# Places in a hand-set order: one offset for four sequences, or a place of its own for each

## The chip, the core and the metric

The kernel runs on one core of one Trainium2 chip. The metric is the device time of one launch, in microseconds, the median of repeated runs. A core has five engines, each with its own queue that it works off strictly in order: PE (TensorE, matmul), ACT (ScalarE), DVE (VectorE), POOL (GpSimd) and SP (SyncE, here only for DMA). They meet through semaphores: an instruction may wait until a counter has a value, and everything behind it in its queue waits with it.

## What is computed

x has four sequences of 512 tokens with 128 features. Each block adds its result to x, after a layer norm of x:

```python
x = x + attn_a(layernorm(x))    # projections, rotary, a state-space scan, gated norm
x = x + ffn(layernorm(x))       # routed feed-forward, first time
x = x + attn_b(layernorm(x))    # time mixing (k, v, r, decaying sums), then channel mixing
x = x + ffn(layernorm(x))       # routed feed-forward again, same weights
```

The feed-forward has eight experts of width 256 and a shared branch. Each token takes its two best experts by softmax, but all nine branches are computed for all tokens and weighted:

```python
hid = silu(x @ w_gate[e]) * (x @ w_up[e])
y = y + w_per_expert[:, e:e + 1] * (hid @ w_down[e])
```

Time mixing: k, v and r are projections of mixtures of h with h one token earlier; two decaying sums over time (a numerator and a denominator, kept in range by a running maximum) are divided, gated with sigmoid(r), projected and added. Channel mixing: relu squared of a 512-wide projection, projected back and gated.

## The kernel before

The first block (to about 119 us) is a phase of its own and stays as it is. Everything else is one phase, `phase_body`. Its backbone is 72 *units*: unit u is branch e = u % 9 of *slot* q = u // 9, and a slot is one sequence of one of the two feed-forwards (slots 0 to 3 the first, 4 to 7 the second). The mixings of sequence s run beside it, after slot s and before slot s + 4.

For a unit's two blocks of 128 hidden features PE makes gate and up (`gate_up`, lines 1644 to 1648, three half-precision products each, since every operand is split into a high and a low half), ACT takes Silu of gate (`gate`, line 1844), DVE multiplies with up (`hidden`, line 2033), ACT makes the high half (`high`, line 1851), POOL the low half (`low`, line 2309), and PE multiplies down two units later (`down`, lines 1671 to 1673); DVE adds that into x with the routing weight (`add`, lines 2051 and 2059) three units later. PE has two banks each for gate and up, so it runs at most one unit ahead of ACT and DVE; `down(u)` waits for the low halves of unit u and for the additions of unit u - 1.

All else is hung into that backbone by four functions `beside(u, place)`, one for each of PE, ACT, DVE and POOL. A *place* is a point within a unit of an engine's queue: on DVE for instance

```python
if u >= 3: add(u - 3)
if u < UNITS:
    beside(u, 0)
    hidden(u, 0)
    beside(u, 1)
    hidden(u, 1)
    beside(u, 2)
```

On POOL places 0 and 1 stand ahead of `low(u - 1, 1)` and `low(u, 0)`; on ACT the order is place 0, first Silu, place 1, high half of the unit before, second Silu, place 2, high half, place 3. Before the change a step of sequence s stands 9 s units after that of sequence 0: `at = u - BRANCHES * s, place`, and then `if at == (16, 0): scan_max(s)`. The steps of routing and of the input norms stand at a fixed branch of each slot.

The steps that the prediction names. Routing of slot q: `logits` (PE), `route_shift`, `route_first`, `route_second`, `route_weigh` (DVE, lines 2081 to 2108) and `route_exp` (ACT). Input of slot q: `apply_x`, `turn_x` (PE, line 1678), `high_x`, `low_x`. Weights of the branches 4 to 8: `split_high` (ACT) and `split_low` (DVE, line 2210). The time mixing of sequence s: statistics of the norms `ln_a`, `ln_b` (DVE, `stats` and `aggregate`), `ln_rstd` (POOL, lines 1478 to 1480), `normalise` (ACT, line 1868), `affine` (POOL, lines 2332 and 2335), `apply_h` makes `hn`, `turn_h`, `step`, `share` (DVE, line 2143), `key`, `receptance`, `value` (PE), `scan_max`, `bounds` and `exponentials` (ACT, with the table for Exp), `scan_den` (line 2172) and `scan_num` (line 2177), the products `first_values` (`e2v`), `second_values` (`y2v`), `denominator` and `numerator` (POOL, lines 2339 to 2360), `divide`, `attend`, `output`, `join`. Channel mixing: `turn_c`, `mix`, `hidden` on PE (line 1772), `relus`, `squares`, `values`, `sigmoid`, `gated`, `add_rkv`. The Exp of the decay (line 2005) makes `w_decay` for all scans.

ACT's functions come from tables: Silu and Exp are in different ones, and a change of function puts an `ACT_TABLE_LOAD` ahead of the instruction.

Of the kernel before, what the change touches and what calls it, by code (L numbers as in the profile page):

```python
# [14 lines left out]
SEQS, SEQ = 4, 512  # L15
# [1483 lines left out]
def phase_body(core, io, lns, moe_x):  # L1499
# [8 lines left out]
    with ExitStack() as ctx:  # L1508
# [122 lines left out]
        def _(pe):  # L1631
# [162 lines left out]
            def beside(u, place):  # L1794

                q, e = divmod(u, BRANCHES)
                if (e, place) == (0, 0) and q < SLOTS:
                    logits(q)
                for s in range(SEQS):
                    at = u - BRANCHES * s, place  # L1800
                    if at == (15, 0):
                        turn_h(s)
                    if at == (16, 0):
                        key(s)
                    if at == (18, 1):
                        receptance(s)
                    if at == (18, 2):
                        value(s)
                    if at == (22, 0):
                        output(s)  # L1810
                    if at == (25, 2):
                        turn_c(s)
                    if at == (28, 2):
                        hidden(s, 0)
                        hidden(s, 1)
                        hidden(s, 2)
                    if at == (29, 0):
                        hidden(s, 3)
                    if at == (29, 2):
                        gate_c(s)  # L1820
                    if at == (30, 1):
                        values(s, (0, 1))
                        values(s, (2, 3))
                if (e, place) == (7, 2) and q + 1 < SLOTS:
                    turn_x(q + 1)
# [15 lines left out]
        def _(act):  # L1841
# [103 lines left out]

            def sigmoid(s):
# [3 lines left out]
            def beside(u, place):  # L1950
                q, e = divmod(u, BRANCHES)
                if (e, place) == (7, 3) and q + 1 < SLOTS:
                    high_x(q + 1)
                if q + 1 < SEQS:
                    if (e, place) == (6, 3):
                        apply_x(q + 1, (0, 1))
                    if (e, place) == (7, 0):
                        apply_x(q + 1, (2, 3))
                elif q + 1 < SLOTS:
                    if (e, place) == (6, 1):  # L1960
                        apply_x(q + 1, (2, 3))
                if q == 0 and FRONT_SPLITS <= e + 2 < BRANCHES and place == 1:
                    split_high(e + 2)
                for s in range(SEQS):
                    at = u - BRANCHES * s, place
                    if at == (11, 3):
                        normalise(s, (0, 1))
                    if at == (12, 1):
                        normalise(s, (2, 3))
                    if at == (14, 1):  # L1970
                        apply_h(s, (0, 1))
                    if at == (14, 2):
                        apply_h(s, (2, 3))
                    if at == (15, 1):
                        copy_h(s)
                    if at == (18, 1):
                        bounds(s)
                    if at == (19, 0):
                        exponentials(s)
                        copy_v(s)  # L1980
                    if at == (20, 1):
                        gate_r(s)
                    if at == (24, 3):
                        apply_c(s, (0, 1))
                        apply_c(s, (2, 3))
                    if at == (26, 0):
                        copy_c(s)
                    if at == (28, 2):
                        relus(s, (0,))
                        squares(s, (0,))  # L1990
                        relus(s, (1,))
                        squares(s, (1,))
                    if at == (28, 3):
                        relus(s, (2,))
                    if at == (29, 1):
                        squares(s, (2,))
                    if at == (29, 2):
                        relus(s, (3,))
                    if at == (29, 3):
# [20 lines left out]
        def _(dve):  # L2020
# [192 lines left out]
            def beside(u, place):  # L2213
                q, e = divmod(u, BRANCHES)
                if (e, place) == (0, 0):
                    route_shift(q)
                if (e, place) == (0, 1):
                    route_first(q)
                if (e, place) == (1, 0):
                    route_second(q)  # L2220
                if (e, place) == (1, 0):
                    route_weigh(q)
                if (e, place) == (6, 0) and SEQS <= q + 1 < SLOTS:
                    apply_x(q + 1, (0, 1))
                if (e, place) == (6, 1) and q < 2:
                    stats(ln_m1, x, q + 2)
                if (u, place) == (7, 0):
                    aggregate(ln_m1, 2, veps_in)
                if (u, place) == (15, 2):
                    aggregate(ln_m1, 3, veps_in)  # L2230
                if q == 0 and FRONT_SPLITS <= e + 2 < BRANCHES and place == 2:
                    split_low(e + 2)
                for s in range(SEQS):
                    at = u - BRANCHES * s, place
# [318 lines left out]
```

## Time and profile before

| what | us |
|---|---|
| three runs | 485.51, 485.63, 485.72 |
| median of the runs | 485.63 |
| span of the profiled execution | 484.0 |
| median less span (launch and end, around the span) | 1.6 |
| PE busy | 458.8 (95%) |
| DVE, ACT, POOL busy | 392.8, 364.4, 361.0 |

The profile gives the span of one execution, from its first to its last instruction; its time outside the span is not listed, so its own time is put at the median of the runs, and the span plus 1.6 us is compared with that. PE's 95% is the time in which some matmul's row is open, and these rows overlap; how much of it is issue at full speed has to be read from the starts of the rows. The other engines each have spare time over the whole span, but they have to be read stage by stage, since the four sequences' mixings start one after the other and overlap in the middle. A row's bracket gives the idle time of the engine before it and what ended it.

### The profile page before, as it was taken

What the parts mean: (1) busy time and instruction counts of PE and PEld (TensorE: products, weight loads), DVE (VectorE), ACT (ScalarE), POOL (GpSimd) and SP (SyncE); (2) the same over time, 40 slices, a digit from 0 to 9 for tenths busy, and PEclk for the clock granted to TensorE, in tenths of its full rate; (3) what the DMA queues carried; (4) which work ended last, traced back from release to release, by engine and by line L of the source; (5) the groups of instructions that cost most, each with busy time, mean ns of one, the idle gap of its engine ahead of it and who ended that gap; (6) DMA issues with size and microseconds to landing.
All of it is one profiled execution on the core that took longest, in us unless ns stands there. A gap on an engine that the chain in (4) does not pass through costs nothing.

```text
span 484.0 us, 10598 instructions
## 1 busy us (share of the span) xinstructions
PE 458.8 (95%) x3666; PEld 317.6 (66%) x3666; DVE 392.8 (81%) x1056; ACT 364.4 (75%) x709; POOL 361.0 (75%) x413
## 2 busy tenths in 40 slices
PE   7998999998999999969999989998999999999996
PEld 6775788986456655626666756575657665766664
DVE  6899888786787859997899899979997867486765
ACT  1799989865887667945999679976897588667652
POOL 4664889998566596798788989698969683575652
PEclk9999999999899999998999999999999999999999
DMA  8001010001310000000000000000000000000000
GB/s 276 21 1 65 2 34 3 1 1 35 100 37 2 1 1 1 3 1 1 2 1 1 1 2 1 0 1 3 2 0 24 1 1 24 0 2 1 23 1 24
DMA packets 7061, 8.51 MB, mean 18 GB/s; under 512 B 608, under 2 KB 5216, under 8 KB 7008
## 3 DMA queue, kind: packets, MB, share of 16 engines
q1 hardware_dynamic: 7008, 7.83, 5.0%
q8 instruction: 30, 0.49, 0.4%
q14 instruction: 23, 0.19, 0.1%
HBM read 6.78 MB, written 1.05 MB: 16 GB/s over the span
## 4 chain that ended last, share of the span: by engine, by line
PE 45%; DVE 10%; POOL 8%; ACT 8%; issue 4%; DVEq 0%; ACTq 0%; POOLq 0%
PE bank L1644 8%; PE bank L1645 8%; PE bank L1648 8%; PE bank L1671 5%; PE bank L1672 4%; PE bank L1673 4%; DVE x L2059 3%; POOL b_hid_lo L2309 2%; DVE b_hid L2033 2%; ACT b_silu L1844 2%; PE bank L1772 1%; PE bank L1789 1%; PE bank L1714 1%; PE bank L1678 1%; ACT b_hid_hi L1851 1%
## 5 line engine op out<-in xcount | busy, mean ns | idle before, releaser
L2309 POOL TENSOR_TENSOR b_hid_lo<-b_hid,b_hid_hi 128x512 f16<-128x512 f32 x143 | 172.8, 1218 | 62.6 <-ACT b_hid_hi L1851 60.8
L2033 DVE SCALAR_TENSOR_TENSOR b_hid<-bank,b_silu 128x512 f32<-128x512 f32 x144 | 97.5, 685 | 38.1 <-ACT b_silu L1844 31.3
L1844 ACT ACTIVATE b_silu<-bank 128x512 f32<-128x512 f32 x144 | 85.7, 596 | 41.7 <-PE bank L1648 39.8
L1644 PE MATMUL bank<-x_hi,wsplit 128*128 128x512 f16 x284 | 108.9, 383 | 1.1 <-DVE b_hid L2033 1.0
L1671 PE MATMUL bank<-wsplit,b_hid_hi 128*128 128x128 f16 x576 | 100.4, 219 | 9.7 <-DVE x L2059 5.6
L1645 PE MATMUL bank<-x_hi,wsplit 128*128 128x512 f16 x284 | 108.9, 383 | 0.0
L1648 PE MATMUL bank<-x_lo,wsplit 128*128 128x512 f16 x284 | 108.6, 383 | 0.0
L1673 PE MATMUL bank<-wsplit,b_hid_lo 128*128 128x128 f16 x576 | 100.5, 219 | 0.0
L1672 PE MATMUL bank<-wsplit,b_hid_hi 128*128 128x128 f16 x576 | 100.4, 219 | 0.0
L1851 ACT CAST b_hid_hi<-b_hid 128x512 f16<-128x512 f32 x144 | 88.1, 611 | 15.7 <-DVE b_hid L2033 15.3
L2059 DVE SCALAR_TENSOR_TENSOR x<-bank,b_w_branch,x 128x128 f32<-128x128 f32 x256 | 71.5, 340 | 7.8 <-PE bank L1673 7.5
L1671 PEld LDWEIGHTS bank<-wsplit,b_hid_hi 128*128 128x128 f16 x576 | 56.4, 98 | 23.4 <-POOL b_hid_lo L2309 10.4
L1672 PEld LDWEIGHTS bank<-wsplit,b_hid_hi 128*128 128x128 f16 x576 | 56.4, 98 | 6.5 <-issue 1.3
L1673 PEld LDWEIGHTS bank<-wsplit,b_hid_lo 128*128 128x128 f16 x576 | 56.5, 98 | 0.0
L1648 PEld LDWEIGHTS bank<-x_lo,wsplit 128*128 128x128 f16 x284 | 28.1, 99 | 34.3 <-issue 1.4
L1644 PEld LDWEIGHTS bank<-x_hi,wsplit 128*128 128x128 f16 x284 | 28.6, 101 | 31.0 <-DVE b_hid L2033 5.3
L1645 PEld LDWEIGHTS bank<-x_hi,wsplit 128*128 128x128 f16 x284 | 28.0, 98 | 27.1 <-issue 5.9
L545 DVE SCALAR_TENSOR_TENSOR xbc<-bank,cols,xbc 128x511 f32<-128x511 f32 (+2 forms) x48 | 35.5, 746 | 2.4 <-ACT xbc L825 1.2
L1151 PE MATMUL bank<-causal,seg_l 128*128 128x128 f32 x128 | 17.1, 278 | 0.2 <-ACT expo L870 0.2
L1844 ACT ACT_TABLE_LOAD x13 | 16.7, 1283 | 0.2
L2185 DVE RECIPROCAL bank<-b_den_r 128x256 f32<-128x256 f32 x8 | 14.0, 1754 | 3.4 <-POOL b_den_r L2352 3.4
L1151 PEld LDWEIGHTS bank<-causal,seg_l 128*128 128x128 f32 x128 | 15.7, 192 | 1.5 <-issue 1.4
(249 smaller groups left out, 927.8 us busy)
## 6 DMA issues: line engine op xcount, KB each, us to landing
moe_raw<-in_moe SPq DMA_DIRECT2D x9, 384.0 KB, 3.1
x<-in_x SPq DMA_DIRECT2D x4, 256.0 KB, 3.9
out<-x SPq DMA_DIRECT2D x3, 256.0 KB, 2.6
rope<-in_rope SPq DMA_DIRECT2D x1, 512.0 KB, 5.9
wzx<-in_wzx SPq DMA_DIRECT2D x1, 386.0 KB, 6.3
b_w_rkvo<-in_w_rkvo SPq DMA_DIRECT2D x1, 256.0 KB, 2.7
b_w_fk<-in_w_fk SPq DMA_DIRECT2D x1, 256.0 KB, 2.8
b_w_fv<-in_w_fv SPq DMA_DIRECT2D x1, 256.0 KB, 3.5
```

The costliest lines, as they stand in the source:

```text
L545: ins = nc.vector.scalar_tensor_tensor(xbc[:, b, t0 + back:t1], conv_ps[b % 2][:, 0:SEQ - back], col(core, "conv_w", TAPS * b + TAPS - 1 - ...
L1644: nc.tensor.matmul(dst, hi, x_hi[:, q % 2, :], start=True, stop=False)
L1645: nc.tensor.matmul(dst, lo, x_hi[:, q % 2, :], start=False, stop=False)
L1648: nc.tensor.matmul(dst, hi, x_lo[:, q % 2, :], start=False, stop=True).then_inc(made, 1)
L1671: nc.tensor.matmul(dst, h_hi, d_hi, start=blk == 0, stop=False)
L1672: nc.tensor.matmul(dst, h_hi, d_lo, start=False, stop=False)
L1673: ins = nc.tensor.matmul(dst, h_lo, d_hi, start=False, stop=blk == FBLK - 1)
L1844: nc.scalar.activation(silu[:, 2 * (u % 2) + blk, :], gate_ps[blk][:, :], ACT.Silu, scale=GU_UNSCALE).then_inc(silu_ready, 1)
L1851: nc.scalar.copy(hid_hi[:, FBLK * (u % 3) + blk, :], hid[:, 2 * (u % 2) + blk, :]).then_inc(hi_ready, 1)
L2033: nc.vector.scalar_tensor_tensor(hid[:, 2 * (u % 2) + blk, :], up_ps[blk][:, :], GU_UNSCALE * H_SCALE, silu[:, 2 * (u % 2) + blk, :], ALU. ...
L2059: ins = nc.vector.scalar_tensor_tensor(x[:, i, :], down_bank(u)[:, P * c:P * (c + 1)], w_branch[:, q % 2, e, c:c + 1], x[:, i, :], ALU.mul ...
L2309: nc.gpsimd.tensor_tensor(hid_lo[:, slot, :], hid[:, 2 * (u % 2) + blk, :], hid_hi[:, slot, :], ALU.subtract).then_inc(lo_ready, 1)
```

## The change

Each step gets a list of (unit, place), one for each sequence or slot, and is called where the list says so. The branches of the old `beside` are split so that steps that stood together have lists of their own. No step is added or taken away, and their arithmetic is the same. Every engine's `beside` changes in this way; two lists of each kind are shown here.

```diff
             def beside(u, place):
-
-                q, e = divmod(u, BRANCHES)
-                if (e, place) == (0, 0) and q < SLOTS:
-                    logits(q)
+                here = u, place
+                for q in range(8):
+                    if here == ((0, 0), (7, 2), (16, 1), (27, 1), (36, 0), (44, 0), (53, 1), (61, 2))[q]:
+                        logits(q)
                 for s in range(SEQS):
-                    at = u - BRANCHES * s, place
-                    if at == (15, 0):
+                    if here == ((15, 0), (24, 0), (33, 0), (41, 1))[s]:
                         turn_h(s)
...
-                if (u, place) == (4, 0):
-                    nc.scalar.activation(w_decay[:], col(core, "decay"), ACT.Exp).then_inc(decay_act, 1)
+                for q in range(8):
+                    if here == ((0, 2), (7, 2), (19, 0), (27, 2), (36, 2), (45, 2), (53, 2), (61, 3))[q]:
+                        route_exp(q)
+                for q in range(1):
+                    if here == ((7, 3),)[q]:
+                        decay(q)
...
+                for q in range(8):
+                    if here == ((2, 0), (10, 1), (19, 0), (27, 2), (36, 2), (45, 2), (54, 0), (65, 1))[q]:
+                        route_second(q)
+                for q in range(8):
+                    if here == ((3, 1), (12, 0), (20, 1), (28, 0), (37, 0), (46, 0), (55, 0), (66, 2))[q]:
+                        route_weigh(q)
...
-                    if at == (19, 0):
+                    if here == ((18, 2), (27, 1), (36, 2), (46, 0))[s]:
                         scan_den(s)
-                    if at == (19, 2):
+                    if here == ((19, 1), (29, 0), (37, 1), (46, 1))[s]:
                         scan_num(s)
...
-                    if at == (11, 2):
+                    if here == ((11, 2), (20, 1), (29, 1), (38, 1))[s]:
                         affine(s, 0)
```

The Exp of the decay becomes a function `decay` with the same instruction. Where the order until now guaranteed that a value was there, the steps now wait for it by name:

```diff
             def divide(s, half):
                 dve.wait_ge(den_ready, s + 1)
+                dve.wait_ge(routed, s + 3)
...
             def first_values(s):
+                pool.wait_ge(expo_ready, 4 * s + 2)
                 pool.wait_ge(v_copied, s + 1)
...
             def second_values(s):
+                pool.wait_ge(expo_ready, 4 * (s + 1))
+                pool.wait_ge(v_copied, s + 1)
...
             def denominator(s, part):
                 if part == 0:
+                    pool.wait_ge(expo_ready, 4 * (s + 1))
...
             def numerator(s, part):
                 if part == 0:
+                    pool.wait_ge(expo_ready, 4 * (s + 1))
...
             def add_x4(s):
+                pool.wait_ge(x4_ready, s + 1)
```

**Where rows move.** In the rows that follow, `b_` marks a tile of this phase, `bank` is a PSUM bank, and brackets hold the semaphores that a row waits for. The lines of the changed kernel are some 3 to 28 higher than those of the kernel before.

On POOL, from the time mixing's products of sequence 0 (unit 18) on. Before:

```order
L2339 TENSOR_TENSOR b_e2v<-b_expo,b_v_sb 128x512 [waits b_v_copied]
L2342 TENSOR_TENSOR b_y2v<-b_expo,b_v_sb 128x512
L2347 TENSOR_TENSOR b_den<-b_expo,b_bb 128x512 [waits b_bb]
L2309 TENSOR_TENSOR b_hid_lo<-b_hid,b_hid_hi 128x512 [waits b_hid_hi,b_pool_step]
L2309 TENSOR_TENSOR b_hid_lo<-b_hid,b_hid_hi 128x512 [waits b_hid_hi]
L2349 TENSOR_TENSOR b_den<-b_den,b_expo 128x512
L2352 TENSOR_TENSOR b_den_r<-b_den,b_e_r 128x512 [waits b_er1,b_pool_step]
L2357 TENSOR_TENSOR b_num<-b_expo,b_aa 128x512 [waits b_aa]
L1478 TENSOR_TENSOR ln_tm_rstd<-ln_tm_veps,mhalf 128x4 [waits b_veps_a,b_pool_step]
L1479 TENSOR_TENSOR ln_tm_nbias<-ln_tm_mv,ln_tm_rstd 128x4 [waits b_pool_step]
L1480 TENSOR_SCALAR ln_tm_nbias<-ln_tm_nbias 128x4 [waits b_pool_step]
```

Now:

```order
L2374 TENSOR_TENSOR b_den<-b_expo,b_bb 128x512 [waits b_bb,b_expo]
L2363 TENSOR_TENSOR b_e2v<-b_expo,b_v_sb 128x512 [waits b_v_copied,b_expo,b_pool_step]
L2376 TENSOR_TENSOR b_den<-b_den,b_expo 128x512
L2332 TENSOR_TENSOR b_hid_lo<-b_hid,b_hid_hi 128x512 [waits b_hid_hi,b_pool_step]
L2368 TENSOR_TENSOR b_y2v<-b_expo,b_v_sb 128x512 [waits b_v_copied,b_expo]
L2379 TENSOR_TENSOR b_den_r<-b_den,b_e_r 128x512 [waits b_er1]
L2385 TENSOR_TENSOR b_num<-b_expo,b_aa 128x512 [waits b_aa,b_expo]
L2332 TENSOR_TENSOR b_hid_lo<-b_hid,b_hid_hi 128x512 [waits b_hid_hi,b_pool_step]
L1478 TENSOR_TENSOR ln_tm_rstd<-ln_tm_veps,mhalf 128x4 [waits b_veps_a]
```

The denominator's first product (`b_den<-b_expo,b_bb`) stands ahead of `b_e2v`, its second product ahead of the low half, and `b_y2v` and the numerator between two low halves; before, three products stood ahead of two low halves and three behind them, with `ln_rstd` next.

On DVE, around the denominator's scan `b_bb` of sequence 0 (units 18 and 19). Before, with the end of the routing of slot 2 ahead of it:

```order
L2106 TENSOR_TENSOR bank<-bank,b_second 128x32
L2107 SCALAR_TENSOR_TENSOR bank<-bank,b_ex 128x32 [waits b_dve_step]
L2108 TENSOR_TENSOR b_w_branch<-bank,b_best 128x4x8 [waits b_dve_step]
L2172 SCALAR_TENSOR_TENSOR b_bb<-b_expo 128x512 [waits b_expo]
L2033 SCALAR_TENSOR_TENSOR b_hid<-bank,b_silu 128x512 [waits b_hid_lo,up_made,b_silu] x2
L2177 SCALAR_TENSOR_TENSOR b_aa<-b_expo,b_e2v 128x512 [waits b_e2v]
L2059 SCALAR_TENSOR_TENSOR x<-bank,b_w_branch,x 128x128 [waits b_down]
L2059 SCALAR_TENSOR_TENSOR x<-bank,b_w_branch,x 128x128 x3
```

Now:

```order
L2177 TENSOR_SCALAR b_e_r<-bank 128x512 [waits b_r_made]
L2185 SCALAR_TENSOR_TENSOR b_bb<-b_expo 128x512 [waits b_expo]
L2072 SCALAR_TENSOR_TENSOR x<-bank,b_w_branch,x 128x128 [waits b_down]
L2072 SCALAR_TENSOR_TENSOR x<-bank,b_w_branch,x 128x128 x3
L2108 SCALAR_TENSOR_TENSOR bank<-bank,b_ex 128x32 [waits b_exp]
L2109 TENSOR_REDUCE b_best<-bank 128x4 [waits b_dve_step]
L2110 TENSOR_TENSOR bank<-bank,b_best 128x32 [waits b_dve_step]
L2111 TENSOR_TENSOR bank<-bank,b_rank 128x32 [waits b_dve_step]
L2083 TENSOR_REDUCE b_best<-bank 128x4 [waits b_dve_step]
```

The scan stands right behind `negative_r` (`b_e_r`), ahead of the additions (`x<-bank,b_w_branch,x`) and of the routing's rows, of which those of `route_weigh` have gone to unit 20.

On ACT, the Exp of the decay. Before, in unit 4:

```order
L1851 CAST b_hid_hi<-b_hid 128x512
L2005 ACT_TABLE_LOAD
L2005 ACTIVATE b_w_decay<-cols 128x1
L1844 ACT_TABLE_LOAD
L1844 ACTIVATE b_silu<-bank 128x512
```

Now, in unit 7:

```order
L1847 ACTIVATE b_silu<-bank 128x512
L1919 ACT_TABLE_LOAD
L1919 ACTIVATE b_ex<-b_shift 128x32
L1854 CAST b_hid_hi<-b_hid 128x512
L1950 ACTIVATE b_w_decay<-cols 128x1
L1847 ACT_TABLE_LOAD
L1847 ACTIVATE b_silu<-bank 128x512
```

It shares one pair of table loads with the routing's Exp (`b_ex<-b_shift`) of slot 1.

## Rows read from the trace of the kernel before

**Rows 1.** Head of the page.

```profile
span 484.0 us, 10598 instructions
```

**Rows 2.** Timeline of PE, unit 44: start us, us, engine, line, operation, tiles.

```profile
343.39 0.38 PE L1644 MATMUL bank<-x_hi,wsplit 128*128 128x512 f16 x1
343.60 0.38 PE L1645 MATMUL bank<-x_hi,wsplit 128*128 128x512 f16 x1
```

**Rows 3.** Who PE waited for: us in total, times, longest us.

```profile
PE bank L1671 <- DVE x L2059: 5.6, 9, 1.8
PE bank L1671 <- POOL b_hid_lo L2309: 4.0, 2, 3.5
...
PE bank L1678 <- ACT b_hn L1876: 1.2, 3, 0.4
PE bank L1644 <- DVE b_hid L2033: 1.0, 2, 0.8
...
PE bank L1772 <- DVE b_w_branch L2108: 0.4, 1, 0.4
```

**Rows 4.** Stages: length, busy of PE, PEld, DVE, ACT, POOL; clock, DMA, GB/s.

```profile
119.00:153.00 34.00, 31.27 (x248) 18.33 (x249) 26.24 (x71) 28.46 (x49) 20.77 (x31) 0.95 0.19 60
153.00:184.00 31.00, 30.12 (x270) 19.14 (x269) 22.93 (x79) 22.07 (x42) 23.30 (x26) 1.00 0.01 1
184.00:205.00 21.00, 20.71 (x174) 12.76 (x172) 19.70 (x62) 17.27 (x32) 14.87 (x15) 1.00 0.01 2
205.00:223.00 18.00, 12.44 (x97) 7.23 (x95) 16.05 (x30) 9.98 (x20) 17.60 (x17) 0.91 0.00 0
...
270.00:289.00 19.00, 17.57 (x149) 10.64 (x147) 17.23 (x58) 12.90 (x28) 17.10 (x21) 1.00 0.01 2
...
322.00:340.00 18.00, 16.57 (x137) 9.85 (x135) 16.54 (x56) 11.90 (x26) 16.10 (x21) 1.00 0.01 2
```

**Rows 5.** Timeline of PE: waits, with idle us and releaser in brackets.

```profile
126.38 0.39 PE L1644 MATMUL bank<-x_hi,wsplit 128*128 128x512 f16 x1 [0.75 <-DVE b_hid L2033]
...
141.30 0.22 PE L1671 MATMUL bank<-wsplit,b_hid_hi 128*128 128x128 f16 x1 [1.01 <-DVE x L2059]
...
149.67 0.22 PE L1671 MATMUL bank<-wsplit,b_hid_hi 128*128 128x128 f16 x1 [0.35 <-DVE x L2059]
...
211.05 0.22 PE L1671 MATMUL bank<-wsplit,b_hid_hi 128*128 128x128 f16 x1 [1.78 <-DVE x L2059]
...
218.59 0.23 PE L1671 MATMUL bank<-wsplit,b_hid_hi 128*128 128x128 f16 x1 [3.45 <-POOL b_hid_lo L2309]
```

**Rows 6.** Timeline of ACT, unit 4: two table loads.

```profile
133.38 1.28 ACT L2005 ACT_TABLE_LOAD   x1
...
134.90 1.28 ACT L1844 ACT_TABLE_LOAD   x1
```

**Rows 7.** Timeline of DVE, units 18 and 19.

```profile
202.24 0.18 DVE L2095 SCALAR_TENSOR_TENSOR bank<-bank,b_ex 128x32 f32<-128x32 f32 x1
...
204.87 1.64 DVE L2172 TENSOR_TENSOR_SCAN b_bb<-b_expo 128x512 f32<-128x512 f32 x1
...
207.63 2.26 DVE L2177 TENSOR_TENSOR_SCAN b_aa<-b_expo,b_e2v 128x512 f32<-128x512 f32 x1
```

**Rows 8.** Timeline of POOL, units 18 to 20.

```profile
207.54 1.26 POOL L2347 TENSOR_TENSOR b_den<-b_expo,b_bb 128x512 f32<-128x512 f32 x1
208.88 3.07 POOL L2309 TENSOR_TENSOR b_hid_lo<-b_hid,b_hid_hi 128x512 f16<-128x512 f32 x2
...
215.84 1.01 POOL L1478 TENSOR_TENSOR ln_tm_rstd<-ln_tm_veps,mhalf 128x4 f32<-128x4 f32 x1
...
217.38 1.16 POOL L2309 TENSOR_TENSOR b_hid_lo<-b_hid,b_hid_hi 128x512 f16<-128x512 f32 x1
```

**Rows 9.** Line 2177, the numerator's scans: ns, minimum, median and maximum of four.

```profile
L2177 DVE TENSOR_TENSOR_SCAN b_aa<-b_expo,b_e2v x4: 1330/1336/2257, 207.6 to 361.4; 128x512 f32<-128x512 f32 x4
```

**Rows 10.** Timeline of ACT, unit 20: normalising begins.

```profile
217.46 0.88 ACT L1868 ACTIVATE b_xn<-x,ln_tm_nbias,ln_tm_rstd 128x128 f32<-128x128 f32 x2 [5.25 <-POOL ln_tm_nbias L1480]
```

More of the change, by code:

```diff
@@ L1823, in beside @@
                         values(s, (2, 3))
-                if (e, place) == (7, 2) and q + 1 < SLOTS:
-                    turn_x(q + 1)
+                for q in range(7):
+                    if here == ((5, 0), (16, 0), (25, 1), (34, 1), (42, 1), (53, 0), (61, 1))[q]:
+                        turn_x(q + 1)
             for u in range(UNITS + 2):
@@ L1944, in squares, with decay @@
                     nc.scalar.square(sq[:, b, :], relu[:, b, :]).then_inc(sq_ready, 1)
+            def decay(_):
+                nc.scalar.activation(w_decay[:], col(core, "decay"), ACT.Exp).then_inc(decay_act, 1)
             def sigmoid(s):
@@ L1950, in beside @@
             def beside(u, place):
[L1951 to L1955, printed above, removed]
+                here = u, place
+                for q in range(7):
+                    if here == ((5, 1), (16, 1), (25, 3), (34, 3), (43, 0), (53, 1), (61, 3))[q]:
+                        high_x(q + 1)
+                for q in range(3):
+                    if here == ((3, 1), (12, 2), (20, 2))[q]:
@@ L1956, in beside @@
                         apply_x(q + 1, (0, 1))
-                    if (e, place) == (7, 0):
+                for q in range(7):
+                    if here == ((4, 2), (15, 3), (24, 2), (34, 0), (42, 0), (51, 1), (60, 1))[q]:
                         apply_x(q + 1, (2, 3))
[L1959 to L1963, printed above, removed]
+                for q in range(5):
+                    if here == ((2, 3), (3, 0), (4, 0), (4, 3), (7, 0))[q]:
+                        split_high(q + FRONT_SPLITS)
@@ L2225, in beside @@
[L2225 to L2232, printed above, removed]
+                here = u, place
+                for q in range(8):
+                    if here == ((0, 1), (7, 2), (18, 1), (27, 1), (36, 1), (44, 2), (53, 1), (61, 1))[q]:
+                        route_shift(q)
@@ L2374, in beside @@
             def beside(u, place):
-                q, e = divmod(u, BRANCHES)
-                if (e, place) == (8, 0) and q + 1 < SLOTS:
-                    low_x(q + 1)
-                if (u, place) == (9, 2):
-                    pool.wait_ge(veps_in, 1)
-                    ln_rstd(nc, core, link, ln_m1, of_seq(2), rstd_in)
-                if (u, place) == (18, 2):
-                    pool.wait_ge(veps_in, 2)
-                    ln_rstd(nc, core, link, ln_m1, of_seq(3), rstd_in)
+                here = u, place
@@ L2384, in beside @@
+                for q in range(7):
+                    if here == ((8, 0), (16, 1), (26, 0), (34, 1), (43, 1), (53, 0), (61, 2))[q]:
+                        low_x(q + 1)
+                for q in range(2):
+                    if here == ((8, 1), (15, 0))[q]:
+                        pool.wait_ge(veps_in, q + 1)
+                        ln_rstd(nc, core, link, ln_m1, of_seq(q + 2), rstd_in)
                 for s in range(SEQS):
-                    at = u - BRANCHES * s, place
-                    if at == (11, 0):
+                    if here == ((10, 2), (20, 0), (28, 2), (37, 1))[s]:
```

157 lines of the change are left out of this document (87 added, 70 removed).

## The prediction

> **What bounds the kernel now.** The profiled execution spans 484.0 us [rows 1]; the runs have a median of 485.63 us, so 1.6 us lie around the span, and I add them back at the end. First view: the timeline of PE in an undisturbed unit. Two gate matmuls that follow each other start 0.21 to 0.22 us apart although each row lasts 0.38 us [rows 2]. So a PE that shows no idle time is issuing as fast as it can, and a wait costs some 0.16 us more than the idle time that the trace shows for it (0.38 less 0.22). Second view: who PE waited for. Over the whole body five kinds hold 12.2 us: 5.6 for DVE's additions, 4.0 for POOL's low halves, the rest for ACT's `hn`, DVE's products and the routing weights [rows 3]; some 0.8 us of the 5.6 belong to the very last unit, which nothing here touches. Third view: the stages. PE lost 34.00-31.27 = 2.7 us in 119 to 153, 0.9 in 153 to 184, 0.3 in 184 to 205, 18.00-12.44 = 5.6 in 205 to 223, and 1.4 in each of 270 to 289 and 322 to 340 [rows 4]. Elsewhere in the body PE lost next to nothing. PE is therefore the bound, and the change can earn only these waits: its matmuls are the same before and after. In the worst stage POOL was busy 17.60 of 18 us and DVE 16.05; in 270 to 289 DVE had 17.23 of 19 [rows 4]. So in the stages that lose, PE waits because another engine's queue is full there, not because of one slow instruction.
>
> What is in reach: 2.1 us in three waits of the first stage (0.75, 1.01 and 0.35 [rows 5]; the other 0.6 us stands at the start of the phase, ahead of every moved step), 0.9, 5.6 and twice 1.4 us. Adding 0.16 per wait makes that 2.6, 1.2 (two waits), 6.0 (three) and twice 2.2 (five each). In 205 to 223 the mean granted clock was 0.91 [rows 4], so 0.09 of 18 us was lost to it: 1.6 us at the lower level (1.2 GHz for 3.2 us). A last wait of 0.4 us for the routing weights costs 0.5. All together **16.3 us**.
>
> **Part by part.**
>
> *Start (119 to 153), reach 2.6, taken 2.4.* ACT loads an activation table for `w_decay` in unit 4 and the Silu table again: 1.28+1.28 us [rows 6]. Now the Exp of `w_decay` stands behind the routing's Exp of unit 7, which has the table in already, so one pair leaves: 24 loads in the body where there were 26. ACT is 2.6 us earlier, and the wait at 141.30 is for an addition that stood behind a product which had waited for ACT. `route_second` and `route_weigh` leave the place ahead of unit 1's first product (now units 2 and 3): the wait at 126.38 was for that product, which now is ready some 0.8 us earlier. Two of the five `split_low` now come before their unit's products, not behind them. What is added in their place: the turn of slot 1 (four transposes) at unit 5 instead of 7, which PE does at either place. I leave 0.2 for a new wait.
>
> *Units 9 to 15 (153 to 184), reach 1.2, taken 1.2.* The statistics of `ln_a` go ahead of unit 11's first product, and the routing's 13 rows no longer stand ahead of unit 10's. So `rstd`, which POOL makes ahead of a low half, comes by more than the 0.55 us that PE waited at 171; and the second norm's `ln_rstd` moves to unit 12, so `hn` is there before PE turns it.
>
> *Units 16 to 22 (184 to 223), reach 7.6 in 205 to 223, taken 3.0.* Here one wait feeds the next. The scan of the denominator stands behind 13 routing rows, from 202.24 to 204.87 [rows 7]; POOL's first product of the denominator starts only at 207.54, and POOL then runs without a pause until the low half at 217.38, for which PE has waited 3.45 us [rows 5, 8]. In the new order the scan stands ahead of the addition and of the routing, so only ACT's two exponentials hold it: 204.87-202.24 = 2.6 us earlier, and some 0.4 more because it no longer runs beside `y2v`. POOL has idle time before 205 (14.87 of 21 us busy [rows 4]), so it can take that work about 3 us earlier, and everything behind moves up with it. The lower bound is nothing: POOL still has the same six products and three low halves, and `route_weigh` now stands ahead of `ln_a`'s statistics (1.2 us later). The upper bound is 7.6, no wait and no drop of the clock. I take 3.0, which is the time by which the row that starts POOL's run moves; the clock I leave as it is, since PE keeps a wait of some 2 us.
>
> *Sequences 2 and 3 (270 to 289, 322 to 340), reach 2.2 each, taken 1.3 each.* Without waits such a stage lasts 19.0-2.2 = 16.8 us, and DVE has 17.23 us of work in it [rows 4]; so at least 0.4 has to leave the stage. It does: the second norm's statistics and aggregation come a unit earlier, `share` two places later, and the sigmoid's table pair stands behind unit 30's first Silu. Bounds 0 and 2.2; I take 1.3, between what DVE's load allows (1.8) and half.
>
> *The wait for the routing weights, reach 0.5, taken 0.4.* The hidden product of sequence 3 goes from unit 55 to 56, the weights are made a place earlier.
>
> *New waits.* POOL waits by name for the exponentials, for `v` and for `x4`, DVE for the routing before it divides. Each names what an earlier row of the same queue, or the order until now, had guaranteed; I cost them at nothing. Behind a wait of POOL stands the next low half, and PE waits for that: this is the price if I am wrong (rival S). SP's queue is unchanged.
>
> Sum: 2.4+1.2+3.0+2.6+0.4 = 9.6 us. 484.0-9.6 = 474.4, and with 1.6 around it **476.0 us**.
>
> **Rivals.**
>
> *All of it.* If no wait is left, 16.3 us go: 467.7+1.6 = 469.3. For it: each wait has its own step moved. Against: POOL's 17.60 of 18.
>
> *The full queues keep theirs.* Then only the start, units 9 to 15 and the routing wait are won: 4.0 us, 481.6. For it: loads of 89% to 98% in the three stages. Against: the stages before them have idle time.
>
> *DVE and POOL meet more often.* The scan of the numerator took 2.26 us at 207.63 where it otherwise takes 1.33 [rows 7, 9], beside a POOL product. If the new order brings two more such meetings in each of four sequences, 8 x 0.93 = 7.4 us come back on DVE's queue: 483.4. For it: scans and mixings now stand where POOL has its own products. Against: the first scan moves to where POOL waits for it. The Trainium skill (SBUF — State Buffer, Who interferes with whom) says that a DVE instruction with two inputs in SBUF and a GpSimd instruction that reads SBUF hold the shared interface one at a time, for the whole instruction. By that rule a meeting costs up to the whole of the other instruction and the sum would be this rival's; the longer row agrees with it.
>
> *S, slower.* `affine(s, 0)` now stands ahead of POOL's low half in units 20, 29 and 38, and waits for four rows of ACT that come up to two places later. Today the normalising begins at 217.46, after 5.25 us of waiting for `rstd` [rows 10]. If it ends later than POOL is free, the low half queues behind it and PE stands as it stood at 218.59: 3.45+0.16 us and 1.6 for the clock, 5.2 in each of three sequences, 15.6 in all: 476.0+15.6 = 491.6. It decides from where normalising, four rows of some 0.44 us, ends after the work that stands ahead of `affine` on POOL. Against: PE has the hidden products of the sequence before in units 28 to 30 and 37 to 39, which cover a late low half; nothing covers unit 20.
>
> *Nothing to see.* A run cannot be told from no change within 0.2%, 1 us. If the jam of 205 to 223 only moves, and the start's gain fills PE's waits further on, the time stays at 485.6.
>
> **How the numbers follow.** Forecast 0.52 (472 to 480), all of it 0.13, full queues 0.13, meetings 0.07, S 0.10, nothing 0.05. Faster: 0.52+0.13+0.13+0.07 = 0.85; same 0.05; slower 0.10. The range reaches from 469.5 to 483.5: it holds the forecast, most of the full gain, the full queues and the meetings, and leaves out S and no change.
>
> **What would show it.** Right: no table load for `w_decay` of its own, no PE wait of a microsecond before 150; the scan of the first denominator within 0.5 us of ACT's second exponential; PE's wait in units 19 to 21 below 3 us in one piece; two waits fewer in sequences 2 and 3. Wrong: a POOL `affine` with a wait for ACT in front of it and a PE wait for a low half behind; scans above 2 us in more than one sequence; a second stretch at the lower clock in the body.

## The result, and the profile after

The changed kernel takes 479.06 us (478.16 to 479.66), the kernel before 485.68 us (485.51 to 486.04): a ratio of 0.9862, interval 0.9844 to 0.988. That is 6.6 us less; 9.6 were forecast, and 479.06 lies within 469.5 to 483.5. The profiled execution spans 477.1 us, 6.9 less than before [rows 1].

TensorE's mean granted clock differs between runs of one kernel (the kernel before took from 484.54 us at a mean clock of 1.0 to 487.06 us at 0.988 beside e1 to e4, the changed kernel from 478.16 at 0.998 to 479.66 at 0.995), so medians are compared, and half a microsecond between single runs says nothing.

The head of the page, and who PE waited for in the body (us in total, times, longest us):

```profile
span 477.1 us, 10616 instructions
```

```profile
PE bank L1671 <- DVE x L2072: 4.2, 4, 1.7
PE bank L1671 <- POOL b_hid_lo L2332: 3.1, 1, 3.1
PE bank L1644 <- DVE b_hid L2046: 1.2, 2, 0.9
PE bank L1644 <- ACT b_silu L1847: 1.0, 1, 1.0
...
```

The waits are fewer and longer than before: four for additions where there were nine, one for a low half where there were two, none for `hn` and the routing weights [rows 3]. The stages, with columns as in [rows 4], show where they went. They are fixed stretches of time: by 213 us the changed kernel is 5 us ahead, so each holds somewhat later work than it did before.

```profile
119.00:153.00 34.00, 32.11 (x273) 20.13 (x274) 26.37 (x74) 28.99 (x50) 19.53 (x31) 1.00 0.18 59
153.00:184.00 31.00, 31.00 (x279) 19.54 (x277) 26.11 (x91) 22.68 (x46) 25.08 (x29) 1.00 0.01 1
184.00:205.00 21.00, 19.96 (x165) 12.27 (x164) 19.67 (x43) 17.49 (x31) 16.98 (x15) 1.00 0.01 3
205.00:223.00 18.00, 14.65 (x117) 9.03 (x118) 16.08 (x50) 9.14 (x19) 16.20 (x19) 0.91 0.00 1
223.00:270.00 47.00, 45.55 (x373) 30.50 (x372) 44.20 (x113) 40.68 (x75) 41.67 (x39) 1.00 0.01 1
270.00:289.00 19.00, 19.00 (x175) 12.71 (x174) 17.73 (x49) 14.93 (x30) 16.79 (x20) 1.00 0.00 1
289.00:322.00 33.00, 31.31 (x249) 20.83 (x246) 31.84 (x79) 28.23 (x49) 26.76 (x26) 1.00 0.00 1
322.00:340.00 18.00, 18.00 (x159) 12.01 (x157) 17.14 (x50) 15.57 (x32) 16.83 (x18) 1.00 0.01 2
```

PE's idle time (length less busy) went from 2.73 to 1.89 us in 119 to 153, from 0.88 to 0 in 153 to 184, from 5.85 to 4.39 in 184 to 223, and from 1.43 to 0 in 270 to 289 and in 322 to 340. New are 1.45 in 223 to 270 and 1.69 in 289 to 322, where PE lost nothing before. These are the remaining large waits, in PE's timeline:

```profile
124.70 0.39 PE L1644 MATMUL bank<-x_hi,wsplit 128*128 128x512 f16 x1 [0.98 <-ACT b_silu L1847]
...
204.91 0.39 PE L1644 MATMUL bank<-x_hi,wsplit 128*128 128x512 f16 x1 [0.91 <-DVE b_hid L2046]
...
213.18 0.23 PE L1671 MATMUL bank<-wsplit,b_hid_hi 128*128 128x128 f16 x1 [3.05 <-POOL b_hid_lo L2332]
...
249.65 0.22 PE L1671 MATMUL bank<-wsplit,b_hid_hi 128*128 128x128 f16 x1 [1.45 <-DVE x L2072]
...
300.73 0.22 PE L1671 MATMUL bank<-wsplit,b_hid_hi 128*128 128x128 f16 x1 [1.69 <-DVE x L2072]
```

Two questions follow: why 3.05 of 3.45 us stayed at the low half of unit 19, and what the waits at 249.65 and 300.73, each for an addition, are.

The first: this is POOL in the new order, then in the old one. A *run* here is a row of products between which POOL does not pause.

```profile
199.34 1.27 POOL L2374 TENSOR_TENSOR b_den<-b_expo,b_bb 128x512 f32<-128x512 f32 x1 [3.03 <-DVE b_bb L2185]
200.69 1.27 POOL L2363 TENSOR_TENSOR b_e2v<-b_expo,b_v_sb 128x512 f32<-128x512 f32 x1
...
208.99 1.16 POOL L2332 TENSOR_TENSOR b_hid_lo<-b_hid,b_hid_hi 128x512 f16<-128x512 f32 x1
210.44 1.01 POOL L1478 TENSOR_TENSOR ln_tm_rstd<-ln_tm_veps,mhalf 128x4 f32<-128x4 f32 x1 [0.30 <-DVE ln_tm_veps L2144]
...
211.97 1.15 POOL L2332 TENSOR_TENSOR b_hid_lo<-b_hid,b_hid_hi 128x512 f16<-128x512 f32 x1
```

```profile
204.16 1.27 POOL L2339 TENSOR_TENSOR b_e2v<-b_expo,b_v_sb 128x512 f32<-128x512 f32 x1 [0.39 <-ACT b_v_sb L1897]
205.38 2.19 POOL L2342 TENSOR_TENSOR b_y2v<-b_expo,b_v_sb 128x512 f32<-128x512 f32 x1
```

The first product of the denominator moved from 207.54 [rows 8] to 199.34, but before the change it was not the start of POOL's run: `e2v` and `y2v` ran from 204.16 on, released by ACT's copy of `v`. Now it is the start, and waits 3.03 us for the scan. So the run starts 204.16-199.34 = 4.8 us earlier, not 8.2. From its start to the second low half of unit 19 it is 211.97-199.34 = 12.6 us now and was 217.38-204.16 = 13.2; the same products, low halves and `rstd` stand in it. In either order ACT releases it, by the copy of `v` before (203.51, now 199.01) and by the exponentials and the scan behind them now (200.90 before, 196.39 now): both came 4.5 us earlier. PE came to the low half 5.0 us earlier (at 213.18-3.05 for 218.59-3.45) and POOL 5.4 earlier, so the wait hardly changed.

The second: DVE in units 27 and 28, ACT's row that `route_second` needs, and the same addition on DVE before the change.

```profile
246.43 0.67 DVE L2046 SCALAR_TENSOR_TENSOR b_hid<-bank,b_silu 128x512 f32<-128x512 f32 x1
247.01 0.19 DVE L2108 SCALAR_TENSOR_TENSOR bank<-bank,b_ex 128x32 f32<-128x32 f32 x1
...
248.38 1.13 DVE L2072 SCALAR_TENSOR_TENSOR x<-bank,b_w_branch,x 128x128 f32<-128x128 f32 x4
```

```profile
246.46 0.21 ACT L1919 ACTIVATE b_ex<-b_shift 128x32 f32<-128x32 f32 x1
```

```profile
250.93 1.11 DVE L2059 SCALAR_TENSOR_TENSOR x<-bank,b_w_branch,x 128x128 f32<-128x128 f32 x4
```

Six rows of `route_second` (247.01 to 248.38) now stand ahead of the addition for which PE waits until 249.65; in unit 36 the same rows, `negative_r` and a scan do (296.39 to 299.49). Before, all of them but `negative_r` stood behind it. They do not wait for ACT here: its row ends at 246.67, and DVE comes to `route_second` at 247.01 without a pause. PE reaches the addition's matmul 5.4 us earlier than before (at 249.65-1.45 = 248.20 for 253.62, where it did not wait), but the addition starts only 250.93-248.38 = 2.6 us earlier.

### The profile page after: what moved, and what is told of

Same layout as the page of the kernel before. It is cut to its first block, busy times and chain, and to the rows that moved or that the text cites. A ratio compares the mean times of both kernels' runs of the same rounds, so it can differ in the third digit from the quotient of the medians.

```text
span 477.1 us, 10616 instructions
## 1 busy us (share of the span) xinstructions
PE 455.1 (95%) x3666; PEld 317.6 (67%) x3666; DVE 396.7 (83%) x1056; ACT 363.3 (76%) x707; POOL 359.0 (75%) x413
## 4 chain that ended last, share of the span: by engine, by line
PE 65%; DVE 5%; ACT 3%; issue 1%; POOL 1%; DVEq 0%; ACTq 0%
PE bank L1644 12%; PE bank L1645 12%; PE bank L1648 12%; PE bank L1671 6%; PE bank L1673 6%; PE bank L1672 6%; PE bank L1789 3%; PE bank L1772 3%; PE bank L1678 1%; PE bank L1714 1%; DVE x L2072 1%; DVE b_hid L2046 1%; PE bank L1699 1%; PE bank L1743 1%; PE bank L1779 1%
## 5 line engine op out<-in xcount | busy, mean ns | idle before, releaser
L2332 POOL TENSOR_TENSOR b_hid_lo<-b_hid,b_hid_hi 128x512 f16<-128x512 f32 x143 | 168.1, 1187 | 50.1 <-ACT b_hid_hi L1854 47.7
L1185 PE MATMUL bank<-xdt,mix 128*128 128x64 f32 x128 | 16.3, 272 | 0.2
L1095 PE MATMUL bank<-normT,wzx 128*128 128x512 f32 x32 | 16.1, 601 | 0.1
```

What stands on the lines that cost most here:

```text
L2332: nc.gpsimd.tensor_tensor(hid_lo[:, slot, :], hid[:, 2 * (u % 2) + blk, :], hid_hi[:, slot, :], ALU.subtract).then_inc(lo_ready, 1)
```

## The experiments

The parts come first, then the term of units 16 to 22, then the two places where an engine's queue may be so full that a wait only moves (a *jam*). "The changed kernel" below is 479.06 us.

**e1 and e2: the parts.** In e1 only the steps that stood in units 0 to 15 have their new place, in e2 those of units 0 to 24; `route_second` in both and `aggregate(ln_a, .)` in e2:

```diff
-if here == ((2, 0), (10, 1), (19, 0), (27, 2), (36, 2), (45, 2), (54, 0), (65, 1))[q]:
+if here == ((2, 0), (10, 1), (19, 0), (28, 0), (37, 0), (46, 0), (55, 0), (64, 0))[q]:
...
-if here == ((11, 0), (20, 2), (29, 0), (38, 0))[s]:
+if here == ((11, 0), (20, 2), (29, 1), (38, 1))[s]:
```

> Only the steps that stood in units 0 to 15 before have their new unit and place; all others stand where they stood. Theory 'terms add up' (each stage's waits are its own): the start gives 2.6 us and units 9 to 15 give 1.2, as the two traces differ there, so 485.7 - 3.8 = 481.9 us. Rival 'the jam takes it' (units 16 to 22 are set by when POOL and ACT get through, so an earlier PE only waits longer there): 484 us or more.

> The steps that stood in units 0 to 24 before have their new place, the later ones the old. Terms add up: 1.3 us below e1 (the waits of units 16 to 22 differ by that much in the two traces), 480.6 us; then the places from unit 25 on are worth only 1.5 us, as the waits that leave in sequences 2 and 3 (4.9) less two new ones (3.5). Rival: the whole of the rest lies here, 479.1 us, and the later places are worth nothing.

e1 took 483.15 us (483.11 to 484.1) and e2 481.08 (480.2 to 482.78), beside 486.02 for the kernel before. So the start and units 9 to 15 are worth 2.9 us, units 16 to 24 another 2.1, and the rest 2.0, or 1.7 if each is set against the kernel before of its own session (486.02 and 485.68). Within that the parts add up; no jam takes the first gain. e1 pays for its mixture: a wait for `share`, which still stands at its old place, and the old wait for the low half:

```profile
184.31 1.10 PE L1714 MATMUL bank<-b_shared_h,b_w_rkvo 128*128 128x512 f32 x2 [1.00 <-DVE b_shared_h L2156]
...
215.51 0.23 PE L1671 MATMUL bank<-wsplit,b_hid_hi 128*128 128x128 f16 x1 [3.46 <-POOL b_hid_lo L2332]
```

**e3: one table pair.** Every step at its old place but `decay`. (What ran is the changed kernel's code with the old places, so its named waits are in it too; they show no row of their own.)

```diff
-if here == ((4, 0),)[q]:
+if here == ((9, 3),)[q]:
```

> The kernel before with one edit: the Exp of w_decay moved behind the routing's Exp of unit 9, so one pair of table loads leaves. Theory 'ACT's 2.6 us are what PE waited for at 141.3': that wait (1.0 us, 1.2 with the pitch) goes, perhaps the one at 149.6 too (0.5): 484.0 to 484.5 us. Rival 'DVE's queue is late by itself' (routing and splits): within 0.3 us of 485.7.

485.13 us (484.46 to 486.37), ratio 0.999, interval 0.9977 to 1.0003: not told from no change. The trace has 24 table loads in the body and no wait at 141. So the wait was for ACT, as held. The profiled execution is e3's slowest (486.37 us): its stage 205 to 223 shows a mean clock of 0.82 where before had 0.91 [rows 4], 1.6 us more lost to the lower level, and the microsecond is used up there. Runs of the same mean clock differ the right way: at 0.996 the six of e3 took 484.46 to 485.38 us, the three of the kernel before 485.32 to 485.54. How much of the microsecond stays is not settled by this.

**e7: the step that sized units 16 to 22.** On e1, only the scan moved:

```diff
-if here == ((19, 0), (28, 0), (37, 0), (46, 0))[s]:
+if here == ((18, 2), (28, 0), (37, 0), (46, 0))[s]:
                         scan_den(s)
```

> e1 (483.15 us) with one step more at its new place: the scan of sequence 0's denominator, ahead of the addition and of the routing rows. The prediction held that POOL's run in units 18 to 20 starts with the scan, so the scan 2.6 us earlier is worth up to 3.0 us: 480.2 us. Rival 'the run starts with e2v, which waits for ACT's copy of v': POOL starts no sooner and has the same work, within 0.4 us of 483.15, or slower by up to 1 as the addition stands behind the scan.

482.4 us (481.51 to 483.35): 0.75 less than e1, not 3.0. PE's wait for the low half is what it was, 3.44 us for 3.46, and `e2v`, still the first of POOL's products, starts at 201.44 for 201.08. The wait for the addition fell from 1.78 to 0.86, and one for a product rose from 0.35 to 0.77:

```profile
184.27 1.10 PE L1714 MATMUL bank<-b_shared_h,b_w_rkvo 128*128 128x512 f32 x2 [0.99 <-DVE b_shared_h L2156]
...
207.41 0.22 PE L1671 MATMUL bank<-wsplit,b_hid_hi 128*128 128x128 f16 x1 [0.86 <-DVE x L2072]
...
214.94 0.29 PE L1671 MATMUL bank<-wsplit,b_hid_hi 128*128 128x128 f16 x1 [3.44 <-POOL b_hid_lo L2332]
```

In the old order of POOL an earlier scan alone does nothing for the low half. (The first row serves the section on why the prediction was right.)

**e4: the additions first.** On the changed kernel:

```diff
-if here == ((2, 0), (10, 1), (19, 0), (27, 2), (36, 2), (45, 2), (54, 0), (65, 1))[q]:
+if here == ((2, 0), (10, 1), (19, 0), (28, 0), (37, 0), (45, 2), (54, 0), (65, 1))[q]:
                         route_second(q)
...
-if here == ((18, 2), (27, 1), (36, 2), (46, 0))[s]:
+if here == ((18, 2), (27, 1), (37, 0), (46, 0))[s]:
                         scan_den(s)
```

> The changed kernel with DVE's route_second of slots 3 and 4 and the scan of sequence 2's denominator behind the additions of units 25 and 34, as before the change, in place of ahead of them. Theory 'rows that wait for ACT stand ahead of an addition that PE waits for': the new PE waits at 249.6 and 300.7 (1.45 and 1.69 us, 3.5 with the pitch) lose 1.4 and 1.85 us: 479.1 - 3.2 = 475.9 us. Rival 'DVE's queue is full there': the next products come later by as much and the waits move on: 478.5 to 479.1 us.

479.28 us: nothing. The waits for the two additions are gone, and PE waits a matmul or a unit later for the routing weights and a product:

```profile
251.10 3.67 PE L1772 MATMUL bank<-b_mixed,b_w_fk 128*128 128x512 f32 x8 [1.16 <-DVE b_w_branch L2121]
...
301.04 2.81 PE L1772 MATMUL bank<-b_mixed,b_w_fk 128*128 128x512 f32 x6 [0.53 <-DVE b_w_branch L2121]
...
310.31 0.39 PE L1644 MATMUL bank<-x_hi,wsplit 128*128 128x512 f16 x1 [0.92 <-DVE b_hid L2046]
```

3.14 us of idle time became 2.61, in three waits instead of two, and the time is the same: the rival, a full DVE queue, holds. My theory of single rows at the wrong place falls.

**e8: the scan behind as well.** e4 with sequence 1's scan behind the weights, and two POOL products with it:

```diff
-if here == ((18, 2), (27, 1), (37, 0), (46, 0))[s]:
+if here == ((18, 2), (28, 0), (37, 0), (46, 0))[s]:
                         scan_den(s)
...
-if here == ((18, 2), (27, 1), (37, 0), (46, 0))[s]:
+if here == ((18, 2), (28, 1), (37, 0), (46, 0))[s]:
                         denominator(s, 0)
-if here == ((19, 0), (27, 2), (37, 0), (46, 0))[s]:
+if here == ((19, 0), (28, 1), (37, 0), (46, 0))[s]:
                         denominator(s, 1)
```

> e4 with sequence 1's scan of the denominator behind the addition and the routing weights of units 28 and 29, and POOL's first two products of that denominator behind the low half that they stood ahead of. In e4 the PE wait at 250.8 is for the weights, and the scan (1.14 us) stands ahead of them: if DVE's order decides, 1.1 us leave: 478.1 us. Rival 'DVE's sum of work decides': the waits add up to what they were, 479.0 to 479.4 us.

482.28 us (480.64 to 483.53), worse by 3. The wait for the weights fell from 1.16 to 0.29 us, but the products came later, and PE waited for what follows from them:

```profile
257.49 1.13 PE L1779 MATMUL bank<-b_w_fr,b_mixed 128*128 128x128 f32 x8 [0.99 <-ACT b_relu L1942]
...
267.44 1.16 PE L1743 MATMUL bank<-b_w_rkvo,b_att 128*128 128x128 f32 x8 [0.88 <-DVE b_att L2204]
```

Its runs also had a lower mean clock (0.989 in three of six), so part of the 3 us is that: in the profiles e8's first product of unit 24 already comes 1.4 us later than e4's, ahead of every moved step (228.81 for 227.45), and that of unit 71 3.1 us later (470.61 for 467.49). The difference, some 1.8 us, is what the edit costs.

**e6: less work for DVE.** `mix` of sequence 1 on 64 columns; the rest of its result is left out:

```diff
-nc.vector.scalar_tensor_tensor(mixed[:, j, :], dif[:], col(core, ("cmk", "cmr")[j]), hcT[:, 0:SEQ],
+n = 64 if s == 1 else SEQ
+nc.vector.scalar_tensor_tensor(mixed[:, j, 0:n], dif[:, 0:n], col(core, ("cmk", "cmr")[j]), hcT[:, 0:n],
```

> The changed kernel, but sequence 1's two mix rows on DVE (0.75 us each, 1.61 beside POOL) make 64 of the 512 columns; the rest of their result is left out. Theory 'DVE is full there, and what it is relieved of PE gets': 1.3 us less ahead of the addition at 299.5, so the PE wait at 300.7 (1.69 us) falls to about 0.4: 477.4 to 477.8 us. Rival 'the wait is for ACT' (exponentials, routing Exp): the addition comes no sooner, 479.1 us.

478.99 us: no gain that shows in the time, but the trace says why. An eighth of the row still takes 1.14 us, where the whole row takes 0.75 with POOL idle (at 244.63 in the changed kernel) and took 1.61 here. The row in the changed kernel; then in e6 DVE, POOL and PE:

```profile
294.25 1.61 DVE L2214 SCALAR_TENSOR_TENSOR b_mixed<-b_dif,cols,b_hcT 128x512 f32<-128x512 f32 x1
```

```profile
294.38 1.14 DVE L2215 SCALAR_TENSOR_TENSOR b_mixed<-b_dif,cols,b_hcT 128x64 f32<-128x64 f32 x1
```

```profile
292.06 3.38 POOL L2333 TENSOR_TENSOR b_hid_lo<-b_hid,b_hid_hi 128x512 f16<-128x512 f32 x3
```

```profile
300.39 0.22 PE L1671 MATMUL bank<-wsplit,b_hid_hi 128*128 128x128 f16 x1 [1.21 <-DVE x L2072]
```

The DVE row ends at 295.52, as POOL's three low halves do (295.44). DVE was relieved of 1.61-1.14 = 0.47 us, and PE's wait fell by 1.69-1.21 = 0.48. So in unit 36 PE gets all that DVE is relieved of.

**e9: a row moved from DVE to ACT.**

```diff
+act.wait_ge(r_made, s + 1)
+nc.scalar.activation(e_r[:], ps_t[:, :], ACT.Relu, bias=80.0).then_inc(neg_r_ready, 1)
 act.wait_ge(neg_r_ready, s + 1)
-nc.scalar.activation(e_r[:], e_r[:], ACT.Exp).then_inc(er_ready, 1)
+nc.scalar.activation(e_r[:], e_r[:], ACT.Exp, scale=-1.0, bias=80.0).then_inc(er_ready, 1)
...
-nc.vector.tensor_scalar(e_r[:], ps_t[:, :], -1.0, 80.0, ALU.mult, ALU.min).then_inc(neg_r_ready, 1)
```

> The changed kernel with DVE's row that negates and bounds the receptance (128x512 out of PSUM, 0.68 us, one in each of four sequences) gone from DVE: ACT does it as a Relu with bias 80 ahead of the Exp, which gets scale -1 and bias 80. Theory 'DVE is full, and what it is relieved of PE gets': 0.6 us in each sequence in which PE waits for DVE (at 204.9, 249.7 and 300.7): 479.1 - 1.2 to 1.8 = 477.3 to 477.9 us. Rival 'ACT's exponentials decide': ACT is 0.6 us longer there and POOL's e2v starts later: 479 to 479.7 us.

479.23 us: nothing in sum. In unit 36, where the row stood within DVE's run, the wait fell from 1.69 to 1.10, by the row's 0.6. Elsewhere ACT, 0.6 longer, took DVE's place: in unit 18 the wait of 0.91 became 0.32 (for ACT) and 0.16, in unit 27 it rose from 1.45 to 1.78, since `route_second` now does wait for its Exp (0.24 us) and the addition stands behind that row, and a wait of 0.36 for `share` is new at 283.06:

```profile
202.21 0.39 PE L1644 MATMUL bank<-x_hi,wsplit 128*128 128x512 f16 x1 [0.32 <-ACT b_silu L1847]
...
249.63 0.22 PE L1671 MATMUL bank<-wsplit,b_hid_hi 128*128 128x128 f16 x1 [1.78 <-DVE x L2074]
...
300.66 0.22 PE L1671 MATMUL bank<-wsplit,b_hid_hi 128*128 128x128 f16 x1 [1.10 <-DVE x L2074]
```

**e5: the low halves of units 19 and 20 first.** On the changed kernel, POOL's table alone:

```diff
-if here == ((10, 2), (20, 0), (28, 2), (37, 1))[s]:
+if here == ((10, 2), (20, 1), (28, 2), (37, 1))[s]:
...
-if here == ((11, 2), (20, 1), (29, 1), (38, 1))[s]:
+if here == ((11, 2), (21, 1), (29, 1), (38, 1))[s]:
                         affine(s, 0)
-if here == ((12, 1), (21, 0), (30, 0), (38, 1))[s]:
+if here == ((12, 1), (21, 1), (30, 0), (38, 1))[s]:
                         affine(s, 1)
...
-if here == ((19, 1), (28, 2), (37, 1), (47, 0))[s]:
+if here == ((20, 1), (28, 2), (37, 1), (47, 0))[s]:
                         numerator(s, 0)
```

> The changed kernel with POOL's order in units 19 to 21 altered: both low halves of unit 19 ahead of numerator(0, .) and of the rstd of ln_a, both of unit 20 ahead of affine(1, .). Theory 'order': PE's 3.05 us at 213.2 are spent on the product of the numerator and the rstd that stand ahead of one low half (1.27 and 1.5 us), and PE gets them back: 2.0 us and perhaps the stretch at the lower clock (0.9 in these runs): 476 to 477 us. Rival 'jam': POOL runs without a pause from 199.3 to 219.8, so the wait moves to the products and low halves behind, within 0.5 us of 479.1.

479.05 us (478.26 to 479.46): the jam. No wait for a low half is left in units 19 and 20, and DVE's rows took its place, the addition of unit 18 and a product of unit 21:

```profile
212.03 0.22 PE L1671 MATMUL bank<-wsplit,b_hid_hi 128*128 128x128 f16 x1 [1.77 <-DVE x L2064]
...
215.80 0.39 PE L1644 MATMUL bank<-x_hi,wsplit 128*128 128x512 f16 x1 [1.63 <-DVE b_hid L2046]
```

In its DVE timeline the addition stands behind a row of four elements in each partition, as long as POOL's product beside it:

```profile
210.10 1.18 DVE L2144 TENSOR_TENSOR ln_tm_veps<-b_v_eps,ln_tm_mv 128x4 f32<-128x4 f32 x1
211.20 0.68 DVE L2064 SCALAR_TENSOR_TENSOR x<-bank,x 128x512 f32<-128x512 f32 x1
211.80 3.36 DVE L2199 RECIPROCAL bank<-b_den_r 128x256 f32<-128x256 f32 x2
```

```profile
210.00 1.26 POOL L2385 TENSOR_TENSOR b_num<-b_expo,b_aa 128x512 f32<-128x512 f32 x1
```

The stretch at the lower clock went as well (mean clock 0.999 or 1.0 in all its runs), and the median stayed. The profile shows somewhat more than the median: PE comes 0.65 us earlier to the waits at 249.65 and 300.73 (249.01 and 300.08), the last write of the output takes 2.40 us for 1.77, and the spans are both 477.1 us. That gain fits the clock and not the order: the waits here grew from 3.05 to 3.40 us.

**e10 and e11.** e10 is e5 with the statistics of `ln_a` at (21, 0) in place of (20, 1) and the second reciprocal at (21, 1) in place of (21, 0); e11 is e10 with e9's edit.

> e5 with three DVE steps of units 20 and 21 moved: the statistics of ln_a behind the addition of unit 18 (PE waited 1.77 us for it at 211.9), and the second reciprocal behind the product of unit 21 (PE waited 1.63 us). If each wait is for what stands ahead of it, both shrink by a microsecond or more: 477 us. Rival 'jam': DVE has no pause from 197.4 to 217, so the waits come back within the same units: 478.5 to 479.3 us.

> e9 and e10 in one kernel. If DVE's sum of work bounds units 16 to 22 and the sequences behind, the reorder gives little and the relief its 1.2 to 1.8 us: 477.3 to 477.9. If both theories of single rows hold, 475.5.

479.06 us (478.77 to 479.72) and 479.46 (479.1 to 481.37). The wait for the addition is gone in e10, and PE waits for a product, for `att` and (0.79 us, at 221.30) for another product, behind the same DVE rows:

```profile
213.62 0.39 PE L1644 MATMUL bank<-x_hi,wsplit 128*128 128x512 f16 x1 [1.27 <-DVE b_hid L2046]
...
216.07 1.16 PE L1743 MATMUL bank<-b_w_rkvo,b_att 128*128 128x128 f32 x8 [1.64 <-DVE b_att L2204]
```

None of the versions beats the changed kernel by more than its runs differ.

## Why the prediction was right, and where it was off

The sign, the bound and the range were right: what was won came out of PE's waits. The size was 3.0 us too high. By parts, 3.6 us were forecast for the start with units 9 to 15, 3.0 for units 16 to 22, and 3.0 for sequences 2 and 3 with the routing wait; e1, e2 and the changed kernel give 2.9, 2.1 and 2.0 (or 1.7).

*Start and units 9 to 15.* The waits at 141.30, 149.67, 171 and 182 are gone, and with them the table pair: 24 loads. At 124.70 PE now waits 0.98 us for ACT's Silu, in place of 0.75 for DVE at 126.38 [rows 5], where 0.2 was left for a new wait. But before, a stretch at the lower clock lay over this place (0.95 in [rows 4]), which the sum left out, and the two cost about the same: e1 has the new order and the stretch (0.95), and none of the new waits; e7 has them and no stretch (1.00); PE comes to the wait for `share` at 184.31 and 184.27.

*Units 16 to 22: the term rested on the wrong row.* "I take 3.0, which is the time by which the row that starts POOL's run moves" took the product at 207.54 for the start. The run began at 204.16 with `e2v`, which waits for ACT's copy of `v`. e7 shows it: the scan alone leaves the low half's wait at 3.44 us. With POOL's new order the scan does start the run, but ACT releases it no earlier for PE than before: it starts 10.8 us ahead of PE's coming to the low half (210.13-199.34), and started 11.0 ahead (215.14-204.16). What the part gained (2.1) goes with the wait for the addition (1.78 to 0.30), `share` in e1, and half a microsecond of POOL's run, less a longer wait for a product at 204.91 (0.91 for 0.35 in e1). The scan did come as foretold, 0.44 us after ACT's second exponential (197.98, less 196.39+1.15); PE's longest wait missed the mark of 3 us by 0.05.

*Sequences 2 and 3: DVE's load was seen and counted in the wrong stage.* The ten waits in 270 to 289 and 322 to 340 are all gone, 2.86 us of idle time, and 3.14 us are back in two waits in the units before, where I counted nothing. The step that was wrong is "it does" (leave the stage): whether the units ahead had room for what moves there was not asked. DVE from its first product of unit 24 to that of unit 30, before and now, and two of its rows of unit 28 now:

```profile
232.77:270.30 37.53, 37.53 (x306) 25.09 (x305) 32.92 (x76) 33.98 (x62) 31.59 (x30) 1.00 0.00 1
```

```profile
227.29:264.54 37.25, 35.80 (x288) 24.07 (x286) 34.85 (x79) 32.36 (x60) 32.00 (x30) 1.00 0.01 1
```

```profile
256.74 1.00 DVE L2143 TENSOR_SCALAR b_v_eps<-ln_tm_mv 128x4 f32<-128x4 f32 x1
257.78 1.18 DVE L2144 TENSOR_TENSOR ln_tm_veps<-b_v_eps,ln_tm_mv 128x4 f32<-128x4 f32 x1
```

DVE is busy 1.9 us more there with hardly more rows; 1.5 of it are these two, which took 0.50 and 0.17 us before (at 262.73 and 263.26) and now run beside POOL's rows. That fills the units behind the first wait. Ahead of it, in units 24 to 27, DVE has the same work as before (22.50 us for 22.33): there the wait is the order, the addition behind a scan and six rows, and e4 shows why another order does not help, since the rows behind it are needed just as soon. What stays of the gain is fewer pieces: eight waits less, at some 0.16 us each. e6 and e9 show, in unit 36, that less work on DVE shortens the wait.

*The routing weights.* Gone, as forecast (0.4).

*New waits.* No PE wait follows from POOL's waits by name. What cost was not in my list: the rows of `route_second`, which need ACT's Exp behind four exponentials (246.46), now stand ahead of an addition. In the changed kernel the Exp is there in time; with ACT 0.6 us longer (e9) it is not.

*The rivals.* S did not come: `affine` of sequences 1, 2 and 3 starts at 214.31, 262.98 and 314.45 without a wait. The full queues kept part of theirs: this rival was the nearest to what happened in units 16 to 22. Of the meetings about half came: DVE's busy time rose by 396.7-392.8 = 3.9 us where the rival had 7.4, and three of four scans of the numerator took 1.97 to 2.14 us, one in [rows 7, 9].

## What to carry to other kernels

Before crediting a step that moves earlier, find the row that starts the unbroken run it belongs to, and what that row waits for: reordering within a run changes who waits, not for how long. When work leaves a full stage, ask whether the rows of the units ahead come as much earlier as the engine that needs them, and compare busy time from unit to unit, not between fixed times. A full queue shows itself by edits of the order that move the waits and leave the time (e4, e5 and e10).

## What the runs showed of the hardware

A DVE row can wait out a whole POOL row. In e5 a `tensor_tensor` on 128x4 took 1.18 us from 210.10 to 211.28, and POOL's product 210.00 to 211.26; the same row takes 0.16 elsewhere. A `mix` on 64 columns ended with POOL's low half (e6). DVE's product rows, which read PSUM and one SBUF tile, stay at 658 to 694 ns in all 144 instances. The Trainium skill (SBUF — State Buffer, Who interferes with whom) says that the ports shared by DVE and POOL are an exclusive lock, and, of DVE's two-port modes, that whoever issues first has them for the whole instruction; these rows agree. I had priced it for long rows; it weighs most on the smallest, of which norms and routing are made.

A stretch at the lower of the two clocks (1.2 GHz) of 3.4 us can cost less than half its length, 1.7 us, where PE would have waited anyway. In the start it cost nothing: e1 with it and e7 without it come to `share` at 184.31 and 184.27. In 205 to 223 it cost about 0.95: the changed kernel has it (0.91) and e2 does not (1.00); they come to the low half's wait at 213.18 and 213.32 and to a matmul of unit 24, with the same matmuls between, at 228.00 and 227.19, and e2 waits 0.57 us at 218.88, where the changed kernel does not wait. The runs agree: beside e1 to e4, three runs of the kernel before with a mean clock of 0.996 took 485.32 to 485.54 us, and three at 1.0 took 484.54 to 484.81. What stays open is why some runs of one kernel have such stretches and others not; PE's wait of 3.05 us does not decide it, since e2 has the same one and no drop behind it.
